# A two-stage transformer kernel on one core: the feed-forward half's second product from fp32r parts, and where weights and rotation tables are loaded

## The chip, the cores and the metric

The kernel runs on one core of one Trainium2 chip. Its time is the device time of one execution in microseconds; the median of several runs counts. Engines are TensorE (PE, with its weight loads as PEld), VectorE (DVE), ScalarE (ACT), GpSimd (POOL) and SyncE (SP), which issues most transfers.

## What is computed

An attention layer without a mask over 2 x 2048 tokens (256 wide, 16 heads of 16), then two layers of local attention and a gated feed-forward half. In float32, cut to what matters:

```python
def _layer(x, wqkv, qs, ksc, wo, lg, lb, w1, b1, w2, b2):      # twice, DEPTH = 2
    h = shift_token(x)                                          # half of the columns from the token before
    q, k, v = split(h @ wqkv)                                   # 8 heads of 64
    q, k = rotary_xpos(l2norm(q) * qs, l2norm(k) * ksc)         # rotation tables by position
    x = x + local_attention(q, k, v) @ wo                       # windows of 128, the one before and its own
    h = layer_norm(shift_token(x)) * lg + lb
    a, g = split(h @ w1 + b1)                                   # 682 columns each
    h = a * gelu(g)
    return x + h @ w2 + b2                                      # w2: 682 x 256
```

## The kernel before

The program has three phases: projection of the first attention, its attention (32 heads, to about 1500 us), and `feed_forward_phase`, which runs the end of the first attention and both local layers, to 2903 us. The order of the work on each engine is written out by hand: every engine has its own loop over `steps`, and semaphores tie them together.

In the third phase a tile is 128 tokens; there are `NT` = 32 tiles a layer and 64 in all. Step `t` handles several tiles at different stages: on TensorE in turn the scores of tile `t + 1` (`scores`, L1222), the projection of `t + 2` (`project`, L1191), the transposes of the probabilities of `t + 1` (L1261), the transpose of the normalised rows of `t` (L1237), outputs of heads of `t + 1` (L1303), transposes of queries and keys of `t + 2` (L1326, which waits for `rotary_done`), the product with `wo` of `t + 1` (L1342), and the transpose of `x` for `t + 3` (L1175).

The feed-forward half is done for a pair of tiles. In an even step TensorE does the first product, `hidden` (L1289), of the pair that begins with `t - 2`: 36 matmuls behind the scores and 30 behind L1237. ScalarE applies the gelu (L1468, L1470) and DVE multiplies (`gated`, L1676); the result, `act_T`, stands in `gate`, six chunks of 256 tokens, of which the last has 64 rows. In the odd step that follows TensorE does the second product, `hidden_out` (L1358), once for each tile of the pair: `hidden_out(t - 3)` behind the scores and `hidden_out(t - 2)` behind L1237. It multiplies `gate` with `w2_sb`, both float32 (the trace shows each such matmul as two instructions). `add_hidden` (L1615) on DVE adds the product to `x_sb`.

The first product and the projection already work with parts: a value is rounded to fp32r ("hi"), the rest is a second fp32r value ("lo"), and hi x hi, hi x lo and lo x hi are summed, three fp32r matmuls for one. Weights are split into such parts by GpSimd during the attention phase, in pieces of 512 columns (`PIECES`, `split_piece`, L556 and L558), and stored in DRAM; SP moves them (`prepare_weights`). The pieces pass through the space of `tables`, where the rotation's cosines and sines are loaded afterwards as a whole (`load_tables`).

The second layer's `wqkv` is loaded in two halves: the high part by SP at the start of the phase, into its own space in `k_stack` (`load_second_wqkv(sp, 0)`), the low part by ScalarE's queue over the first layer's low part, once the first layer's last projection is done (`t + 2 == NT - 1`).

On DVE the step's order is: maxima of the scores (L1584), split of the transposed `x` (L1603), reciprocals (L1592), statistics of the middle rows (L1622 to L1627, which wait for a DMA that shifts rows of `x_mid`), normalisation of two groups of probabilities (L1598), cosines of queries and keys (L1641, both wait for ScalarE's `squares_made`), normalised rows (L1634), copy of transposed probabilities (L1655), square norms (L1649), the second copy, rotation (L1662, L1663), scaling of the keys by the inverse norm (L1669). On ScalarE: exponentials (L1427), copies and squares of queries and keys (L1438, L1439), copies of transposed probabilities (L1448), L1456, in even steps the gelu, then copies L1476, L1481, L1483 and the rounding of transposed `x` (L1488, L1490). On GpSimd: normalisation of two groups of probabilities (L1046), L1051, addition of the bias (L1056), sines (L1067, two instructions), inverse norms (L1074, L1076, a power), the split of the first product's input (L1084, L1086), and every second step the rotation's tables (L1039).

Of the kernel before, what the change touches and what calls it, by code (L numbers as in the profile page):

```python
# [13 lines left out]
P = 128  # L14
# [369 lines left out]
def attention_phase(nc, ins, division, VO, mask_sb, weights, ident, load_output_weights, stacks, qkT_stored):  # L384

    with ExitStack() as ctx:
# [3 lines left out]
        q_stack, k_stack, q_minus_first = stacks.q, stacks.k, stacks.q_minus  # L390
        v_ones = sb("v_ones", [P, BODY, TB, VW])
        probs = sb("probs", [P, PROBS, 512])
        excess = probs[:, PROBS - BLOCKS:].rearrange("p (i k) c -> p i k c", i=2)
        spare_pieces = weights.tables[:].rearrange("p a t h d -> p (a t h d)").rearrange("p (i c) -> p i c", c=PIECE)
        raw_piece, piece_hi, piece_lo = spare_pieces[:, 0], spare_pieces[:, 1].bitcast(F32R), spare_pieces[:, 2].bitcast(F32R)
# [61 lines left out]
        def _(sp):  # L457
# [33 lines left out]
            for n in range(NH):  # L491
# [16 lines left out]
                if n == TABLES_HEAD:  # L508
                    sp.wait_ge(weights.parts_stored, 32 * (len(PIECES) - IN_PLACE))
                    weights.load_tables(sp, ins)  # L510
# [9 lines left out]
        def _(pool):  # L520
# [23 lines left out]
            def split_piece(i):  # L544
# [3 lines left out]
                if i < IN_PLACE:  # L548
                    _, _, k, columns = PIECES[i]
                    hi, lo = weights.wqkv_hi[0][:, k, columns], weights.wqkv_lo[:, k, columns]  # L550
# [154 lines left out]
        def _(dve):  # L705
# [70 lines left out]
          + [("w1", l, k, slice(a, min(a + PIECE, W1_COLUMNS))) for l in range(LAYERS) for k in range(NC) for a in range(0, W1_COLUMNS, PIECE)])  # L776
# [3 lines left out]
class Weights:  # L780


    def __init__(self, nc, ctx, stacks):
# [5 lines left out]
        self.wqkv_hi = [sb("wqkv2_hi0", [P, NC, 3 * INNER], F32R)]  # L789
        self.wqkv_lo = sb("wqkv2_lo", [P, NC, 3 * INNER], F32R)  # L790
        self.tables = sb("tables2", [P, 2, TB, 2, D2 // 2])
# [8 lines left out]
        self.tables_loaded, self.small_loaded = sem("tables2_loaded"), sem("small2_loaded")  # L800
        self.wqkv1_loaded, self.w1_loaded, self.wo_loaded, self.w2_loaded = (sem(n) for n in ("wqkv2_1_loaded", "w1_2_loaded", "wo2_loaded", "w2_loaded"))

    def place_wide(self, ctx, stacks):
# [5 lines left out]
        self.w2 = sb("w2_sb", [P, HC, C])  # L809

    def place_second(self, in_k):

        self.wqkv_hi.append(in_k(NC, 3 * INNER))

    def raw_piece(self, ins, i):
        name, l, k, columns = PIECES[i]
        return ins[name][l].rearrange("(k p) n -> p k n", p=P)[:, k, columns]

    def stored_piece(self, i, part):
        name, l, k, columns = PIECES[i]  # L820
        return self.wqkv_parts[part, :, k, columns] if name == "wqkv2" else self.w1_parts[l, part, :, k, columns]

    def load_tables(self, eng, ins):
        for i, name in enumerate(("cos2", "sin2")):
            eng.dma_start(self.tables[:, i], ins[name].rearrange("(t p) (a d) -> p t a d", p=P, a=2)).then_inc(self.tables_loaded, 16)
# [18 lines left out]
    def load_w2(self, eng, ins, l):  # L844
# [13 lines left out]
def feed_forward_phase(nc, ins, weights, stacks, division, x_sb, outputs, spare, wo1_loaded, x1_dram, mask_sb, ident, out):  # L858

    with ExitStack() as ctx:  # L860
# [162 lines left out]
        def _(pool):  # L1023
# [109 lines left out]
            for t in steps:  # L1133
# [17 lines left out]
                if exists(t):  # L1151
                    split_y(t)
# [749 lines left out]
```

## Time and profile before

| | us |
|---|---|
| median of three runs | 2899.72 |
| the three runs | 2899.66, 2899.72, 2905.52 |
| the profiled execution, whole | 2905.26 |
| its span | 2903.4 |
| busy in it: PE, DVE, ACT, POOL | 2807.7, 2323.1, 2113.7, 960.1 |

A row of a timeline gives the start, the length, the engine and line, the tiles written and read with their shapes, the count of instructions merged into it, and in brackets the idle time before it with what ended it. On TensorE instructions overlap, so that their pace is read from starts and not from lengths. Names are those of the memory, not of the view: `VO` holds queries, keys, probabilities and rotated values, `k_stack` the split of `x`, `q_minus_first` and `q_stack` the first product's operands, `tables_small` small columns and the rotation's tables, `wo_bo_sb` the normalised rows.

### The profile page before, as it was taken

The numbers are of one execution on the slowest core, as the hardware profiler recorded it, in microseconds if no ns is written. First come the engines' busy times: TensorE is split into PE (matmuls) and PEld (weight loads), VectorE is DVE, ScalarE is ACT, GpSimd is POOL, SyncE is SP. The second block draws the span as 40 slices with busy tenths as digits, with TensorE's granted clock in tenths as the row PEclk, the third lists the DMA queues.
The fourth block names the chain that finished last, engine by engine and source line by source line (L and its number), as shares of the span: only waits on it lengthen the run. The fifth ranks groups of instructions, "written<-read, shape, count | busy, mean of one in ns | idle before, by whom it ended". The sixth has DMA issues, their size and how long they took to land. (4 is left out here: it accounts for less than half of the span.)

```text
span 2903.4 us, 59150 instructions
## 1 busy us (share of the span) xinstructions
PE 2807.7 (97%) x22608; PEld 1755.0 (60%) x22608; DVE 2323.1 (80%) x4287; ACT 2113.7 (73%) x4556; POOL 960.1 (33%) x1102
## 2 busy tenths in 40 slices
PE   7999999999999999999997899999999999999997
PEld 7743333333333333333355788888887788888886
DVE  7779999999999999999816677777776677777774
ACT  5568888888888888888856566666666676666763
POOL 7600000010001000000016555555555555656553
PEclk9869999999999999999998899999999999999999
DMA  5613334443444243424203000000000100000000
GB/s 164 189 18 53 52 46 60 62 72 59 70 61 72 55 68 60 74 43 66 42 22 128 11 5 4 5 5 4 5 4 34 54 12 19 19 19 11 20 18 25
DMA packets 85944, 131.33 MB, mean 45 GB/s; under 512 B 33120, under 2 KB 59168, under 8 KB 78240
## 3 DMA queue, kind: packets, MB, share of 16 engines
q1 hardware_dynamic: 79376, 120.41, 21.1%
q10 hardware_dynamic: 6288, 7.14, 0.8%
q8 instruction: 181, 2.97, 0.5%
q14 instruction: 99, 0.81, 0.1%
HBM read 83.98 MB, written 34.61 MB: 41 GB/s over the span
## 5 line engine op out<-in xcount | busy, mean ns | idle before, releaser
L684 ACT ACTIVATE probs<-scores 128x512 f32<-128x512 f32 x2048 | 1114.7, 596 | 199.2 <-PE scores L610 76.3
L717 DVE TENSOR_REDUCE mx<-aux 128x1 f32<-128x1024 f32 x982 | 1201.1, 1223 | 61.4 <-PE aux L578 54.1
L578 PE MATMUL aux<-k_stack,q_stack 48*128 48x512 f32 x2006 | 757.4, 453 | 6.4 <-DMA k_stack<-qk_dram 4.1
L610 PE MATMUL scores<-q_stack,k_stack 50*128 50x512 f32 x2048 | 762.5, 450 | 0.0
L623 PE MATMUL pv<-probs,v_ones 128*32 128x256 f32 x8192 | 658.5, 393 | 0.1
L610 PEld LDWEIGHTS scores<-q_stack,k_stack 50*128 50x128 f32 x2048 | 310.2, 186 | 428.8 <-ACT probs L684 411.2
L623 PEld LDWEIGHTS pv<-probs,v_ones 128*32 128x32 f32 x8192 | 161.7, 108 | 361.5 <-ACT probs L684 289.4
L578 PEld LDWEIGHTS aux<-k_stack,q_stack 48*128 48x128 f32 x2006 | 306.4, 188 | 38.0 <-DVE mx L717 19.2
L531 POOL CAST m_parts<-head_max 128x16 fp32r<-128x16 f32 x32 | 6.3, 198 | 938.6 <-DVE head_max L710 938.6
L1427 ACT ACTIVATE VO<-VO,tables_small 128x256 f32<-128x256 f32 (+1 forms) x512 | 250.9, 492 | 48.7 <-DVE tables_small L1584 48.5
L1289 PE MATMUL bank<-q_minus_first,q_stack 128*128 128x256 f32 x2112 | 268.5, 285 | 0.6 <-DVE x_sb L1615 0.6
L1289 PEld LDWEIGHTS bank<-q_minus_first,q_stack 128*128 128x128 f32 x2112 | 256.5, 191 | 11.0 <-issue 10.9
L1584 DVE CUSTOM_DVE_ANT_0 VO<-bank,mask_sb,tables_small 128x256 f32<-128x256 f32 (+1 forms) x512 | 216.1, 469 | 52.0 <-PE bank L1222 52.0
L1046 POOL TENSOR_TENSOR VO<-VO,tables_small 128x512 f32<-128x512 f32 (+1 forms) x128 | 127.3, 1015 | 347.9 <-DVE tables_small L1592 347.9
L1067 POOL TENSOR_TENSOR VO<-VO,tables_small 128x512 f32<-128x512 f32 x128 | 166.1, 1319 | 99.2 <-issue 99.2
L1358 PE MATMUL bank<-w_sb,gate 128*128 128x256 f32 (+1 forms) x768 | 195.8, 397 | 1.3 <-DVE gate L1676 1.1
L1076 POOL TENSOR_TENSOR tables_small<-tables_small 128x16 f32<-128x16 f32 x64 | 189.6, 2962 | 5.3
L1358 PEld LDWEIGHTS bank<-w_sb,gate 128*128 128x128 f32 (+1 forms) x768 | 137.6, 192 | 47.4 <-issue 31.7
L1191 PE MATMUL bank<-wqkv_lo,k_stack 128*128 128x512 f32 x384 | 152.2, 396 | 0.0
L1476 ACT COPY oT<-bank 128x512 f32<-128x512 f32 x64 | 37.6, 587 | 155.5 <-PE bank L1303 155.5
L1438 ACT COPY VO<-bank 128x512 f32<-128x512 f32 x128 | 75.1, 587 | 83.9 <-PE bank L1191 83.9
L1191 PE MATMUL bank<-wqkv_hi,k_stack 128*128 128x512 f32 x384 | 128.6, 402 | 5.2 <-DVE tables_small L1584 2.7
(173 smaller groups left out, 4334.9 us busy)
## 6 DMA issues: line engine op xcount, KB each, us to landing
q_stack<-qk_dram SPq DMA_DIRECT2D x192, 128.0 KB, 5.1
k_stack<-qk_dram SPq DMA_DIRECT2D x192, 128.0 KB, 7.2
qk_dram<-qkT_hi SPq DMA_DIRECT2D x32, 256.0 KB, 3.7
qk_dram<-qkT_lo SPq DMA_DIRECT2D x32, 256.0 KB, 3.8
VO<-o_stage SPq DMA_DIRECT2D x128, 32.0 KB, 6.9
q_minus_first<-sums_dram SPq DMA_DIRECT2D x32, 128.0 KB, 2.9
w_parts<-tables SPq DMA_DIRECT2D x16, 256.0 KB, 2.5
x_dram<-x_sb SPq DMA_DIRECT2D x16, 256.0 KB, 2.0
```

The lines of the kernel that those rows point to most:

```text
L578: return nc.tensor.matmul(out, q_stack[max_rows, n % BODY, tile * P:(tile + 1) * P], k_stack[max_rows, n % BODY, keys * 512:(keys + 1) * 512],
L610: last = nc.tensor.matmul(out, k_stack[0:SCORE_ROWS, n % BODY, s * P:(s + 1) * P], q_stack[0:SCORE_ROWS, n % BODY, j * 512:(j + 1) * 512], ...
L623: last = nc.tensor.matmul(pv[VW * j:VW * (j + 1), columns], v_ones[:, n % BODY, s, :], probs[:, (BLOCKS * step + j) % PROBS, columns], sta ...
L684: nc.scalar.activation(probs[:, e % PROBS], scores[:, item_of_exp(e) % BANKS1], ACT.Exp, scale=float(D1) ** -0.5).then_inc(act_emptied, 1)
L717: nc.vector.tensor_reduce(mx[:, n % BODY, tile, half:half + 1], aux[:, unit % 2].rearrange("p a k -> p (a k)"), AX.X, ALU.max).then_inc(dv ...
L1067: last = nc.gpsimd.tensor_tensor(out=o4[:, :, :, lo:lo + D2 // 2], in0=q4[:, :, :, hi:hi + D2 // 2], in1=sin_table[:, v // 2 % 2, :, lo:lo ...
L1076: nc.gpsimd.tensor_tensor(out=rnorm[:, v % 2], in0=norm2_min, in1=minus_half, op=ALU.pow).then_inc(rnorm_made, 1)
L1191: last = nc.tensor.matmul(bank[QKV_BANK[a]][:], x_part[:, v % 4, k, tokens], w_part[:, k, columns], start=(k == 0 and n == 0), stop=(k == ...
L1289: last = nc.tensor.matmul(out_half, w_part[:, k, chunk * P:(chunk + 1) * P], h_part[:, p % 2, k], start=(k == 0 and n == 0), stop=(k == NC ...
L1358: last = nc.tensor.matmul(bank[F_BANK[v % 2]][:, 0:C], act_T[rows, c, v % 2 * P:(v % 2 + 1) * P], w2_sb[rows, c], start=(c == 0), stop=(c ...
L1427: last = nc.scalar.activation(probs[j][:, u, keys], probs[j][:, u, keys], ACT.Exp, scale=-1.0, bias=negmax[:, j, u:u + 1], accum_out=sums[ ...
L1584: last = nc.vector.tensor_tensor_reduce(out=probs[j][:, u, at:at + n_keys], in0=src[:, 2 * u * P + at:2 * u * P + at + n_keys], in1=mask_s ...
```

## The change

`w2` is split into parts like the other weights: six more pieces, stored as `w2_parts`, loaded as `w2_hi` and `w2_lo`. `hidden_out` now sums three products (act_hi x w2_hi, act_hi x w2_lo, act_lo x w2_hi), 18 fp32r matmuls for six float32 ones. The parts of the activation are new tiles in `k_stack`: ScalarE rounds `gate` to `act_hi` in two halves of three chunks (`round_hidden`), and GpSimd subtracts (`split_hidden`). The missing rows of the last chunk are zeroed once. `gelu` of a pair waits for the subtraction of the pair before, where it waited for its second product.

To make room, the second layer's `wqkv` has no space of its own: both parts are loaded by ScalarE's queue in the layer change, over the first layer's. The pieces have a buffer of their own (`weight_pieces`), and the rotation's tables only hold two pairs: SP loads those of a pair in the odd step `t` for pair `(t + 5) // 2`.

```diff
+PIECES ... + [("w2", l, None, slice(a, a + PIECE)) for l in range(LAYERS) for a in range(0, HC * C, PIECE)]
...
-        act_T = gate
+        act_hi, act_lo = in_k(HC, 2 * P), in_k(HC, 2 * P)
...
             weights.load_first(sp, ins)
-            weights.load_second_wqkv(sp, 0)
             for t in steps:
+                if t % 2 == 1 and exists(t + 5):
+                    p = (t + 5) // 2
+                    sp.wait_ge(tables_made, 2 * (p - 1))
+                    weights.load_tables(sp, ins, p)
...
             def rotary_tables(p):
+                pool.wait_ge(weights.tables_loaded[p % 2], 32 * (p // 2 + 1))
...
+            def split_hidden(p):
+                for i in range(2):
+                    chunks = slice(i * HC // 2, (i + 1) * HC // 2)
+                    pool.wait_ge(act_high_made, 2 * p + i + 1)
+                    nc.gpsimd.tensor_tensor(out=act_lo[:, chunks], in0=gate[:, chunks], in1=act_hi[:, chunks], op=ALU.subtract).then_inc(act_split, 1)
...
             def hidden_out(v):
-                pe.wait_ge(act_made, HC * (v // 2 + 1))
...
-                for c in range(HC):
-                    rows = slice(0, P if c < HW else HR)
-                    last = nc.tensor.matmul(bank[F_BANK[v % 2]][:, 0:C], act_T[rows, c, v % 2 * P:(v % 2 + 1) * P], w2_sb[rows, c], start=(c == 0), stop=(c == HC - 1))
+                out, tokens = bank[F_BANK[v % 2]][:, 0:C], slice(v % 2 * P, (v % 2 + 1) * P)
+                for i, (a_part, w_part) in enumerate(((act_hi, w2_hi), (act_hi, w2_lo), (act_lo, w2_hi))):
+                    for c in range(HC):
+                        if c % (HC // 2) == 0 and i != 1:
+                            pe.wait_ge(act_high_made if i == 0 else act_split, 2 * (v // 2) + c // (HC // 2) + 1)
+                        rows = slice(0, P if c < HW else HR)
+                        last = nc.tensor.matmul(out, a_part[rows, c, tokens], w_part[rows, c], start=(i == 0 and c == 0), stop=(i == 2 and c == HC - 1))
...
             def gelu(p):
-                        act.wait_ge(F_done, 2 * p)
+                        act.wait_ge(act_split, 2 * p)
...
+            def round_hidden(p, i):
+                chunks = slice(i * HC // 2, (i + 1) * HC // 2)
+                act.wait_ge(act_made, HC * p + chunks.stop)
+                if i == 0 and p:
+                    act.wait_ge(F_done, 2 * p)
+                nc.scalar.copy(act_hi[:, chunks], gate[:, chunks]).then_inc(act_high_made, 1)
...
                     if t + 2 == NT - 1:
-                        weights.load_second_wqkv(act, 1)
+                        weights.load_second_wqkv(act)
```

On TensorE, in the odd step, in the kernel before: the scores, the early second product and the first projection matmuls.

```order
L1175 MATMUL bank<-ident,x_sb 128x128 x2
L1222 MATMUL bank<-VO,qT 128x256 x8
L1358 MATMUL bank<-w_sb,gate 128x256 x6
L1191 MATMUL bank<-wqkv_hi,k_stack 128x512
L1191 MATMUL bank<-wqkv_lo,k_stack 128x512
```

The same place on TensorE in the changed kernel:

```order
L1190 MATMUL bank<-ident,x_sb 128x128 x2
L1237 MATMUL bank<-VO,qT 128x256 x8
L1376 MATMUL bank<-w_hi,k_stack 128x256 x6
L1376 MATMUL bank<-w_lo,k_stack 128x256 x6
L1376 MATMUL bank<-w_hi,k_stack 128x256 x6
L1206 MATMUL bank<-wqkv_hi,k_stack 128x512
L1206 MATMUL bank<-wqkv_lo,k_stack 128x512
```

Nothing moved here; one row of six became three rows of six, the activation's parts being in `k_stack`.

On ScalarE, from the gelu of an even step to the load of the exponential's table, in the kernel before (at the layer change, where a weight load on this queue also stands):

```order
L1468 ACT_TABLE_LOAD
L1468 ACTIVATE gate<-bank,b_sb 128x256 x5
L1470 ACTIVATE gate<-bank,b_sb 64x256
L1476 COPY oT<-bank 128x512
L1481 COPY qT<-bank 128x512
L1483 COPY VO<-bank 128x512
L1488 CAST k_stack<-bank 128x2x128
L1490 CAST k_stack<-bank 128x1
L838 DMA wo_sb<-in_wo 128x4x256
L1427 ACT_TABLE_LOAD
```

The same place on ScalarE in the changed kernel:

```order
L1486 ACT_TABLE_LOAD
L1486 ACTIVATE gate<-bank,b_sb 128x256 x5
L1488 ACTIVATE gate<-bank,b_sb 64x256
L842 DMA q_stack<-w_parts 128x2816 x2
L1502 COPY oT<-bank 128x512
L1507 COPY qT<-bank 128x512
L1509 COPY VO<-bank 128x512
L1497 CAST k_stack<-gate 128x768
L1514 CAST k_stack<-bank 128x2x128
L1516 CAST k_stack<-bank 128x1
L1497 CAST k_stack<-gate 128x768
L1445 ACT_TABLE_LOAD
```

Two casts of 128x768 were put in, one ahead of the rounding of `x` and one between it and the load of the exponential's table.

On GpSimd, from the end of an even step to the odd step's first instructions, in the kernel before:

```order
L1084 CAST q_minus_first<-wo_bo_sb 128x2x128
L1086 TENSOR_TENSOR q_minus_first<-wo_bo_sb,q_minus_first 128x2x128
L1046 TENSOR_TENSOR VO<-VO,tables_small 128x512 x2
L1051 TENSOR_TENSOR tables_small<-tables_small 128x1
L1056 TENSOR_TENSOR x_sb<-x_mid,q_minus_first 128x256
```

The same place on GpSimd in the changed kernel:

```order
L1090 CAST q_minus_first<-wo_bo_sb 128x2x128
L1092 TENSOR_TENSOR q_minus_first<-wo_bo_sb,q_minus_first 128x2x128
L1099 TENSOR_TENSOR k_stack<-gate,k_stack 128x768 x2
L1052 TENSOR_TENSOR VO<-VO,tables_small 128x512 x2
L1057 TENSOR_TENSOR tables_small<-tables_small 128x1
L1062 TENSOR_TENSOR x_sb<-x_mid,q_minus_first 128x256
```

The two subtractions stand between the split of an even step and the normalisation of the odd one.

## Rows read from the trace of the kernel before

**Rows 1.** Busy time by stretch, one of a hundred microseconds in the settled part
```profile
1900.00:2000.00 100.00, 98.84 (x733) 84.71 (x733) 71.97 (x208) 64.11 (x166) 55.04 (x57) 1.00 0.02 5
```

Its columns are the stretch, its length, busy time of PE, PEld, DVE, ACT and POOL with their instructions, granted clock, DMA share and GB/s.

**Rows 2.** TensorE's timeline over one odd step
```profile
2135.91 2.00 PE L1222 MATMUL bank<-VO,qT 64*128 64x256 f32 x16
2137.84 3.05 PE L1358 MATMUL bank<-w_sb,gate 128*128 128x256 f32 x12
2140.82 0.50 PE L1191 MATMUL bank<-wqkv_hi,k_stack 128*128 128x512 f32 x1
...
2147.09 2.97 PE L1358 MATMUL bank<-w_sb,gate 128*128 128x256 f32 x12
...
2152.34 1.09 PE L1326 MATMUL bank<-ident,VO 128*128 128x128 f32 x8 [0.39 <-DVE VO L1669]
...
2155.31 2.00 PE L1222 MATMUL bank<-VO,qT 64*128 64x256 f32 x16
```

**Rows 3.** TensorE's waits from 1560 us on: total, times, longest
```profile
PE bank L1326 <- DVE VO L1669: 17.2, 33, 2.3
```

**Rows 4.** DVE's timeline in the same odd step
```profile
2144.06 0.68 DVE L1641 TENSOR_TENSOR VO<-bank,tables_small 128x512 f32<-128x512 f32 x1
2145.05 0.69 DVE L1641 TENSOR_TENSOR VO<-bank,tables_small 128x512 f32<-128x512 f32 x1 [0.31 <-ACT VO L1439]
2145.66 0.43 DVE L1634 TENSOR_SCALAR wo_bo_sb<-x_mid,tables_small 128x256 f32<-128x256 f32 x1
2146.20 0.69 DVE L1655 COPY PT<-bank 128x512 f32<-128x512 f32 x1
...
2151.49 0.80 DVE L1669 TENSOR_TENSOR VO<-VO,tables_small 128x512 f32<-128x512 f32 x1 [1.67 <-POOL tables_small L1076]
```

**Rows 5.** TensorE's timeline in the even step before
```profile
2116.81 4.56 PE L1289 MATMUL bank<-q_minus_first,q_stack 128*128 128x256 f32 x36
2121.21 0.39 PE L1191 MATMUL bank<-wqkv_hi,k_stack 128*128 128x512 f32 x1
```

**Rows 6.** ScalarE's timeline around the odd step; last row, a group by line
```profile
2134.11 0.59 ACT L1483 COPY VO<-bank 128x512 f32<-128x512 f32 x1
...
2136.47 1.28 ACT L1427 ACT_TABLE_LOAD   x1
2138.00 0.51 ACT L1427 ACTIVATE VO<-VO,tables_small 128x256 f32<-128x256 f32 x1 [0.25 <-DVE tables_small L1584]
...
2142.53 0.59 ACT L1438 COPY VO<-bank 128x512 f32<-128x512 f32 x1 [0.43 <-PE bank L1191]
...
2143.93 0.59 ACT L1438 COPY VO<-bank 128x512 f32<-128x512 f32 x1 [0.31 <-PE bank L1191]
...
L352 ACT CAST bqkv_parts<-bqkv_sb 128x768 fp32r<-128x768 f32 x1 | 0.8, 826 | 0.0
```

**Rows 7.** GpSimd: one group by line, then single rows of its timeline
```profile
L558 POOL TENSOR_TENSOR tables<-tables 128x512 fp32r<-128x512 f32 x14 | 18.0, 1286 | 1.1
...
2858.42 0.74 POOL L1086 TENSOR_TENSOR q_minus_first<-wo_bo_sb,q_minus_first 128x256 fp32r<-128x256 f32 x1
...
2151.82 1.05 POOL L1086 TENSOR_TENSOR q_minus_first<-wo_bo_sb,q_minus_first 128x256 fp32r<-128x256 f32 x1
...
2140.14 2.04 POOL L1046 TENSOR_TENSOR VO<-VO,tables_small 128x512 f32<-128x512 f32 x2 [6.99 <-DVE tables_small L1592]
```

**Rows 8.** A transfer's issue (KB, us to landing); DVE's timeline in step 34
```profile
wqkv_lo<-wqkv_parts ACTq DMA_DIRECT2D x1, 1536.0 KB, 6.4
...
2288.69 0.49 DVE L1622 BATCH_NORM_STATS2 tables_small<-x_mid 128x6 f32<-128x128 f32 x2 [3.72 <-DMA x_mid<-x_mid]
```

**Rows 9.** GpSimd's sines of rows 4's step; DVE and GpSimd at the layer change
```profile
2144.64 2.58 POOL L1067 TENSOR_TENSOR VO<-VO,tables_small 128x512 f32<-128x512 f32 x2 [1.06 <-issue]
...
2269.53 1.39 DVE L1634 TENSOR_SCALAR wo_bo_sb<-x_mid,tables_small 128x256 f32<-128x256 f32 x1
...
2267.82 2.95 POOL L1067 TENSOR_TENSOR VO<-VO,tables_small 128x512 f32<-128x512 f32 x2
```

More of the change, by code:

```diff
@@ L390, in attention_phase @@
         q_stack, k_stack, q_minus_first = stacks.q, stacks.k, stacks.q_minus
+        pieces = sb("weight_pieces", [P, 3, PIECE])
         v_ones = sb("v_ones", [P, BODY, TB, VW])
@@ L508, in _ @@
                 if n == TABLES_HEAD:
-                    sp.wait_ge(weights.parts_stored, 32 * (len(PIECES) - IN_PLACE))
-                    weights.load_tables(sp, ins)
+                    for p in range(2):
+                        weights.load_tables(sp, ins, p)
                 if n == TABLES_HEAD + 1:
@@ L799, in __init__ @@
         self.b2_dram, self.b2_copied = nc.dram_tensor("b2_copy", (LAYERS, C), F32).ap(), sem("b2_copied")
-        self.tables_loaded, self.small_loaded = sem("tables2_loaded"), sem("small2_loaded")
+        self.tables_loaded, self.small_loaded = [sem(f"tables2_loaded{i}") for i in range(2)], sem("small2_loaded")
         self.wqkv1_loaded, self.w1_loaded, self.wo_loaded, self.w2_loaded = (sem(n) for n in ("wqkv2_1_loaded", "w1_2_loaded", "wo2_loaded", "w2_loaded"))
@@ L842, in load_w1, with load_w2 @@
             eng.dma_start(self.w1[part].bitcast(F32), self.w1_parts[l, part]).then_inc(self.w1_loaded, 16)
-    def load_w2(self, eng, ins, l):
-        eng.dma_start(self.w2[:], ins["w2"][l].rearrange("(k p) n -> p k n", p=P)).then_inc(self.w2_loaded, 16)
+    def load_w2(self, eng, l):
+        for part in range(2):
+            eng.dma_start(self.w2[part][:].rearrange("p k n -> p (k n)").bitcast(F32), self.w2_parts[l, part]).then_inc(self.w2_loaded, 16)
     def load_first(self, eng, ins):
@@ L1152, in _ @@
                     split_y(t)
+                if t % 2 == 0 and exists(t - 2):
+                    split_hidden((t - 2) // 2)
                 if exists(t + 3) and (t + 3) % 2 == 0:
@@ L1182, in project @@
                     pe.wait_ge(weights.wqkv1_loaded, 32)
-                hi, lo = wqkv_hi[layer(v)], wqkv_lo
+                hi, lo = wqkv_hi, wqkv_lo
                 for a in range(3):
@@ L1348, in hidden_out @@
                 if v % NT == 0:
[L1349 to L1350 removed]
+                    pe.wait_ge(weights.w2_loaded, 32 * (layer(v) + 1))
                 if v % 2 == 0:
@@ L1558, in _ @@
                     copy_qT_kT(t + 2)
+                if t % 2 == 0 and exists(t - 2):
+                    round_hidden((t - 2) // 2, 0)
                 if t >= 0 and exists(t + 3):
                     round_xT(t + 3)
+                if t % 2 == 0 and exists(t - 2):
+                    round_hidden((t - 2) // 2, 1)
                 p = finished_pair(t)
```

58 lines of the change are left out of this document (30 added, 28 removed).

## The prediction, made before the changed kernel ran

> **What bounds the kernel now.** I read the busy time by stretch first, then TensorE's timeline over two steps of the feed-forward phase, then its waits, then the other three engines' timelines over the same step. In the settled part of the phase TensorE is busy 98.84 of 100 us at full granted clock [rows 1]. So taking work from TensorE pays, unless something else is as late as it is. The reader is to look for that something in the one step that the change shortens.
>
> Steps come in pairs. The even step of a pair holds a pair's first product (`hidden`), the odd one both second products (`hidden_out`): one right behind the scores, at 2137.84, one behind the transposes, at 2147.09 [rows 2]. The odd step is 19.4 us long, scores to scores (2135.91 to 2155.31) [rows 2]. Behind its late product TensorE waits 0.39 us, until 2152.34, for DVE's scaled keys [rows 2]; such waits are 17.2 us in all, 33 times, the largest entry of its list [rows 3]. In the even step it never waits there. So the odd step has a second chain that already ends last.
>
> That chain does not pass through the late product. It starts at the projection of the tile two ahead and runs: ScalarE's copy and square of the keys, DVE's cosines (L1641, 2145.05), its normalisation (L1634, 2145.66), a copy of probabilities (L1655, 2146.20), square norms, GpSimd's power, DVE's scaling (L1669, 2151.49), TensorE's L1326 [rows 4]. From 2146.20 to 2152.34 (6.14 us) nothing in it waits for a product.
>
> **The change part by part.**
>
> *The product itself.* Before, 12 instructions in 2.98 us (2137.84 to 2140.82); the late one, at 2147.09, shows 2.97 [rows 2]. After, 18 fp32r instructions of the form 128x128 by 128x256, the form of L1289: 36 of these take 4.40 us (2116.81 to 2121.21), 0.122 us each [rows 5]. 18 x 0.122 = 2.20 us. So each product is 0.75 us shorter (two a pair, 64 in all, 48 us of TensorE time).
>
> *The late product's 0.75 us* is lost: it lies ahead of the 0.39 us wait, which becomes about 1.1 us. Gain 0.
>
> *The early product's 0.75 us* moves the projection forward by that, and the chain hangs on the projection; what else is it late for? DVE: it runs without a pause from the scores' maxima to the first cosines at 2144.06 [rows 4]. The start-to-start time of such an instruction is about 0.61 (2145.05 to 2145.66), so DVE is free for the second cosines at 2144.67 and not before. Today it starts them at 2145.05 after 0.31 us of idling for ScalarE. Then L1634 at 2145.28, and L1655 0.35 later at 2145.63 (its transpose would be there at 2146.20 - 0.75 = 2145.45). That is 0.57 us earlier than 2146.20, and the rest of the chain follows: **gain 0.57 us an odd step**, not 1.5.
>
> *ScalarE's two roundings* (`round_hidden`, 128x768 each, once a pair). A cast of 128x768 took 0.826 us; the next instruction starts some 0.1 us before such an end (as DVE's 2145.05 is 0.69 long and followed at 0.61 [rows 4]), so about 0.70 of the engine each [rows 6]. The first stands behind the keys' copy of 2134.11 and ends at 2135.4, where the engine waited for TensorE anyway. The second stands ahead of the load of the exponential's table, 1.28 us at 2136.47; exponentials began at 2138.00 after a short wait for DVE [rows 6]. Now: 2136.47 + 0.70 + 1.28 = 2138.45, that is 0.45 later. The engine idled 0.43 us before the queries' copy of 2142.53 [rows 6], so it is free at 2142.10 + 0.45 = 2142.55. Copy, square, then the keys' copy at 2143.53 instead of 2143.93, its square done at 2144.6: just ahead of the 2144.67 at which DVE is free. Cost nil beside DVE, with 0.05 us to spare; from there each further 0.1 us on ScalarE takes 0.1 from the gain.
>
> *GpSimd's two subtractions* (`split_hidden`, 128x768). 128x512 took 1.286, 128x256 alone 0.74: 2.13 ns an element, so 1.83 us each [rows 7]. The first can run 2135.5 to 2137.3, the second 2137.35 to 2139.2, where GpSimd stood idle until 2140.14 (normalisation) [rows 7]. TensorE wants the second one after 15 of the early product's 18 matmuls: 2137.84 + 1.83 = 2139.67. Covered by 0.45 us. The other bound: beside DVE's scaling the 256 form took 1.05, not 0.74 [rows 7]; at 4.1 ns an element that is 3.15 us each. I take 1.83, because what DVE runs from 2135.5 to 2139.2 reads PSUM and one SBUF operand, where the slowed row stood beside a product of two SBUF operands.
> The Trainium skill (SBUF — State Buffer, Who interferes with whom) says that GpSimd and DVE share a port pair under an exclusive lock, taken by DVE instructions with two SBUF inputs or in a two-port mode only. By that rule the sum stays at 1.83; by the slowed row taken for all of DVE's instructions it would be the second rival below.
>
> *Waits.* `gelu` now waits for the subtraction of the pair before, a step old: nil. GpSimd's queue behind the subtractions holds only the next normalisation, due at 2140.14: nil while they end before. The second rounding has only the table load behind it.
>
> *Tables pair by pair.* Two 32 KB loads on SP in odd steps, ahead of the next shift of `x_mid`; the wait before them is for tables made two steps earlier, and their reader comes two steps later. Nil.
>
> *Six more weight pieces* in the attention phase: six subtractions of 1.29 us [rows 7] and six casts on GpSimd, which idles there (its busy share is 0 to 1 tenth in those slices of the page); nil, as for the 24 before.
>
> *One-off places.* (a) Opening: 0.75 MB less ahead of the first shift; at the pace of (b) 3.2 us of transfer: gain 0 to 3, I take 1. (b) `wqkv` whole at the layer change: the low half landed in 6.4 us [rows 8]; both, sent at 2185.7, land within 13 us, by 2199, and the projection needs them at 2202. Nil, or 1 us if it hits a shift. (c) Second-layer `w2` is 1.5 MB for 0.75; DVE already waited 3.72 us at 2288.69 for a shift behind it [rows 8]; another 0.75 MB is about 2 us more: loss 2. (d) The end: the last pair's rounding (0.8) and subtraction (1.8) stand in the open, less 1.5 us of TensorE: loss 1.
>
> *Sum.* 31 x 0.57 = 17.7 gained, 2 to 3 us lost net in the one-off places: **15.5 us less**. Against the profiled execution (span 2903.4, run 2905.3) that gives 2889.8. Of the three runs shown two lie at 2899.7 and one at 2905.5, as the profiled one; against the median 2899.7 it gives **2884**.
>
> **The rivals.**
>
> 1. *All of TensorE's time counts*: 31 x 1.5 = 46 us, 2854. It needs the second chain to have slack, and the wait of 0.39 us in every odd step says that it has none. 5%.
>
> 2. *The subtractions come too late* (slower). At 3.15 us each the second ends at 2141.8, the product at 2142.15 instead of 2140.82, and projection, DVE's addition of the product and the chain follow: 1.3 us x 31 = +41, 2940. At 2.6 us each it is +0.4 x 31 = 2912. It decides from where both together take over 4.9 us. 8%.
>
> 3. *DVE misses its turn beside GpSimd* (slower). L1634 starts 1.02 us after GpSimd's sines (L1067, 2.58 us for two), inside the first of them, and takes 0.43. At the layer change it came at 2269.53, 1.71 behind, just past the first, and took 1.39 [rows 9]: shut out by the second. The sines follow the keys' copy, L1634 follows DVE. If the copy is early by all of TensorE's 0.75 (ScalarE not held up as I reckon), the sines start at 2143.9 and L1634 comes at 2145.28, 1.4 later, past the first's end at 1.29; it is then done near 2146.5 to 2146.8 and L1655 is 0.25 to 0.55 later than today: +8 to +17, 2907 to 2917. By my times the sines start at 2144.24 and L1634 comes 1.04 later, 0.25 us inside. Since the margin is small: 15%. The page named above has this rule, that whoever is second waits for the whole instruction; the 1.39 us agree.
>
> 4. *ScalarE takes the gain*: if the second rounding and the table load hold it 0.35 to 0.6 us longer than I reckon, the keys' square is last and 0 to 0.2 us a step remain: 31 x 0 to 0.2 less the 2.5 us of the one-off places, 2896 to 2902. 10%.
>
> Forecast as worked out: 62%, own range 2874 to 2894 (gain per step 0.3 to 0.8, one-off places by 4 us either way, and whether the runs fall low or 6 us high).
>
> **Numbers.** Predicted 2884. The range 2872 to 2908 holds the forecast, rival 4 and the lower end of rival 3; left out are rivals 1 and 2 and the rest of 3. A measurement of this kernel tells about 0.2% (6 us) from no change. Faster by more: forecast and rival 1, less the forecast's edge: 0.65. Within: rival 4 and edges: 0.13. Slower: rivals 2 and 3 with theirs: 0.22.
>
> **What would show it.** Right: the odd step near 18.8 us (scores to scores) for 19.4, the even one unchanged; TensorE's wait at L1326 near 1.3 us in each odd step, 40 us in all; DVE's second cosines with no idle time before them; no wait of the second product for GpSimd; subtractions near 1.83. Wrong: a wait inside the early product (rival 2), L1634 over 1 us long in odd steps (rival 3), DVE idle before the second cosines (rival 4), or no wait at L1326 (rival 1).

## The result, and the profile after

The changed kernel is slower: 2925.5 us median of five runs (2918.0 to 2929.0) against 2899.7 us (2897.0 to 2905.5), a ratio of 1.0083 with a 95% interval of [1.0063, 1.0103]. The forecast was 2884 us, its range 2872 to 2908. The profiled execution of the changed kernel has a span of 2923.7 us, 20.3 us more than that of before (25.8 by the medians: the profiled execution of before took 2905.3 us).

Only a part of these spans bears on the change. The time from the first scores to the end is 1342.1 us before and 1361.6 us in the changed kernel, 19.4 more. A kernel that differs from before in the order of the first product alone (e3_before_spread) has 1342.5. The time ahead of the first scores, in which the change adds little but the splitting of `w2`, goes from 1552.8 to 1575.1 us in the ten traces of this case, at a mean granted clock of 0.99 in the shortest and 0.97 in the longest. Of the 7.1 us between the traces of before and of e3_before_spread 6.8 lie there. So single steps are compared by the traces, and whole times by the ratios of many runs.

In the changed kernel `scores` is L1237, the first product L1304, the projection L1206, the second product L1376, the transposes of the rotated keys L1341, `split_hidden` L1099, `round_hidden` L1497. TensorE's timeline over one odd step (start, length, engine and line, tiles, count; the projection's rows lie between the early product's three rows and the late one's, of which the first stands here):

```profile
2140.36 2.00 PE L1237 MATMUL bank<-VO,qT 64*128 64x256 f32 x16
2142.28 1.17 PE L1376 MATMUL bank<-w_hi,k_stack 128*128 128x256 f32 x6
2143.38 1.16 PE L1376 MATMUL bank<-w_lo,k_stack 128*128 128x256 f32 x6
2144.47 1.16 PE L1376 MATMUL bank<-w_hi,k_stack 128*128 128x256 f32 x6
...
2151.76 1.15 PE L1376 MATMUL bank<-w_hi,k_stack 128*128 128x256 f32 x6
...
2155.02 1.20 PE L1318 MATMUL bank<-PT,VO 128*64 128x128 f32 x18
```

Six matmuls of the product take 1.10 us (2142.28 to 2143.38), 0.183 each, where `hidden`'s take 0.122 [rows 5]. The early product takes 3.29 us (the next projection matmul starts at 2145.57) instead of 2.98 [rows 2], the late one 3.26 (2151.76 to 2155.02) instead of 2.90. The forecast was 2.20. So the product from fp32r parts is longer than the float32 one.

The weight loads show why. Rows of TensorE's weight loads in the same early product, each read in a window of its own, so that a load can stand in two of them (x2): the last two full chunks, the last chunk (64 rows), and the first two of the next part:

```profile
2142.63 0.30 PEld L1376 LDWEIGHTS bank<-w_hi,k_stack 128*128 128x128 f32 x2
...
2142.75 0.19 PEld L1376 LDWEIGHTS bank<-w_hi,k_stack 128*128 128x128 f32 x1
...
2143.07 0.18 PEld L1376 LDWEIGHTS bank<-w_hi,k_stack 64*128 64x128 f32 x1
...
2143.38 0.30 PEld L1376 LDWEIGHTS bank<-w_lo,k_stack 128*128 128x128 f32 x2
```

Loads of full chunks start 0.12 us apart (2142.63, 2142.75). The 64-row chunk's load starts 0.32 us behind its predecessor, and the next 128-row one 0.31 us behind it. At 0.117 these two distances would be 0.23 together; they are 0.63. One visit to the 64-row chunk between chunks of 128 rows, called a stay here, costs 0.40 us, and the part-by-part order makes three stays in a product: 18 x 0.117 + 3 x 0.40 = 3.3 us.

The waits tell the same. One of TensorE's waits (total, times, longest) in the changed kernel, over the whole trace:

```profile
PE bank L1341 <- DVE VO L1699: 7.1, 5, 2.3
```

Over the whole trace of before the wait for the scaled keys was 18.4 us in 34 times; it is 7.1 in 5. (From 1560 us on it was 17.2 in 33 [rows 3], and it is 5.9 in 4.) The late product, 0.36 us longer, has eaten the 0.39 us of each odd step.

Where the 20.3 us are, from the starts of the scores in the two traces: +0.30 in each of 28 settled odd steps (8.4), 0.00 to 0.02 in the even ones; +3.3 in the odd step of the layer change, +0.2 in the next odd one; +2.5 in the step behind the second layer's `w2` load; +5.1 behind the last scores; +0.7 in the opening and ahead of it; some 0.2 in even steps and rounding.

### The profile page after: what moved, and what is told of

The parts are those of the page before. It is cut to its first block and busy times, and to the rows that moved or that the text cites. A ratio compares the mean times of both kernels' runs of the same rounds, so it can differ in the third digit from the quotient of the medians.

```text
span 2923.7 us, 60204 instructions
## 1 busy us (share of the span) xinstructions
PE 2835.1 (97%) x22992; PEld 1784.6 (61%) x22992; DVE 2324.0 (79%) x4287; ACT 2160.8 (74%) x4620; POOL 1087.3 (37%) x1179
## 5 line engine op out<-in xcount | busy, mean ns | idle before, releaser
L1304 PE MATMUL bank<-q_minus_first,q_stack 128*128 128x256 f32 x2112 | 271.7, 287 | 0.6 <-DVE x_sb L1645 0.6
L1304 PEld LDWEIGHTS bank<-q_minus_first,q_stack 128*128 128x128 f32 x2112 | 259.7, 193 | 10.9 <-issue 10.8
L1206 PE MATMUL bank<-wqkv_hi,k_stack 128*128 128x512 f32 x768 | 256.4, 401 | 6.7 <-DVE tables_small L1614 4.1
L1206 PEld LDWEIGHTS bank<-wqkv_hi,k_stack 128*128 128x128 f32 x768 | 145.4, 189 | 43.2 <-issue 4.3
L1376 PE MATMUL bank<-w_hi,k_stack 128*128 128x256 f32 (+1 forms) x768 | 152.2, 318 | 2.3 <-ACT k_stack L1497 1.4
L1206 PE MATMUL bank<-wqkv_lo,k_stack 128*128 128x512 f32 x384 | 152.2, 396 | 0.0
L1099 POOL TENSOR_TENSOR k_stack<-gate,k_stack 128x768 fp32r<-128x768 f32 x64 | 116.7, 1844 | 89.5 <-ACT k_stack L1497 89.5
```

The lines of the kernel that those rows point to most:

```text
L1206: last = nc.tensor.matmul(bank[QKV_BANK[a]][:], x_part[:, v % 4, k, tokens], w_part[:, k, columns], start=(k == 0 and n == 0), stop=(k == ...
L1304: last = nc.tensor.matmul(out_half, w_part[:, k, chunk * P:(chunk + 1) * P], h_part[:, p % 2, k], start=(k == 0 and n == 0), stop=(k == NC ...
L1376: last = nc.tensor.matmul(out, a_part[rows, c, tokens], w_part[rows, c], start=(i == 0 and c == 0), stop=(i == 2 and c == HC - 1))
```

## The experiments

Two theories stood against each other. **Height**: what costs is changing between weights (stationary operands) of 128 and of 64 rows. **Load**: a matmul whose stationary operand is not that of the one before costs 0.183 us (`hidden` uses `w1_hi` twice running, so its mean would be 0.122). A third: these matmuls are slow for where their operands lie.

### All 128 rows in the last chunk: e5_full_rows

```diff
-                        rows = slice(0, P if c < HW else HR)
+                        rows = slice(0, P)
```

> The changed kernel, with all 128 rows of the last chunk of the activation and of w2 in the second product (rows 64 to 127 are zeros in all of them). Theory H (height): in the trace of the changed kernel the weight loads inside a part product start every 0.117 us, but the load of the 64-row chunk starts 0.32 us after its predecessor, and the next 128-row one 0.31 us after it: 0.40 us for each stay at 64 rows, three of them in a product. Without them a product should take 18 x 0.117 = 2.1 us instead of 3.3, each odd step should be about 0.57 us shorter than before the change (the chain over VectorE then sets it, as predicted), and TensorE should wait about 1.1 us for the scaled keys in it. One-off places stay: 2899.7 + 11 - 31 x 0.57 = about 2893. Rival L (load): a matmul whose stationary operand isn't that of the one before it costs 0.183 us, so the product stays at 3.3 and the time at 2925. Rival O: these matmuls are slow for their operands' place, also 2925.

Measured: 2885.0 us, ratio to the kernel before 0.9932 [0.9910, 0.9954], and the odd step is 0.69 to 0.74 us shorter than before in 26 of the 28 settled ones. The expectation of 2893 was too high: the step gained more than 0.57, and part of the changed kernel's losses at the layer change and the end are gone too. Loads, TensorE and its wait:

```profile
2136.59 0.19 PEld L1376 LDWEIGHTS bank<-w_hi,k_stack 128*128 128x128 f32 x1
2136.70 0.19 PEld L1376 LDWEIGHTS bank<-w_lo,k_stack 128*128 128x128 f32 x1
...
2146.37 0.19 PEld L1376 LDWEIGHTS bank<-w_hi,k_stack 128*128 128x128 f32 x1
2146.69 0.14 PEld L1318 LDWEIGHTS bank<-PT,VO 128*64 128x64 f32 x2
...
2149.77 1.09 PE L1341 MATMUL bank<-ident,VO 128*128 128x128 f32 x8 [1.11 <-DVE VO L1699]
...
PE bank L1341 <- DVE VO L1699: 39.2, 34, 2.3
```

The last chunk of one part is followed by the first of the next after 0.11 us (2136.59, 2136.70); from the first of the 18 loads to the one behind the last it is 2.12 us (2136.00 to 2138.12), and from matmul to matmul 2.23. The wait at L1341 is 39.2 us in all; the prediction said 40 for a 2.20 us product. Height holds; load and place fall, since neither order nor place was changed.

The third and fourth row show a limit of the name. Behind the late product, now 128 rows throughout, come the outputs of heads (L1318), whose weights have 128 rows and 64 columns. Their first load starts 0.32 us behind the last full chunk's, as one of 64 rows does. So the change to weights of 64 columns costs as much as one of the rows: loads of 128 x 128 that follow others of that shape from another line (L1252, then L1376) are 0.11 us apart in the changed kernel, so it is not the change of line. No run varies the columns alone. For this the late product, to the start of L1318, takes 2.32 us and not 2.12. VectorE's timeline in the same step:

```profile
2142.12 1.28 DVE L1671 TENSOR_TENSOR VO<-bank,tables_small 128x512 f32<-128x512 f32 x2
2143.32 0.40 DVE L1664 TENSOR_SCALAR wo_bo_sb<-x_mid,tables_small 128x256 f32<-128x256 f32 x1
2143.64 0.68 DVE L1685 COPY PT<-bank 128x512 f32<-128x512 f32 x1
```

Both cosines run without a pause (x2), the normalisation takes 0.40 us and is not shut out, and the copy starts 9.56 us behind the scores (2134.08); before it was 10.29 (2146.20 less 2135.91) [rows 2, 4]. That is 0.73 us, against a forecast of 0.57: the 0.57, 0.11 for first cosines that come 8.04 instead of 8.15 us behind the scores, and a few hundredths behind them.

### The 64-row chunk once a product: e2_by_chunk

```diff
-                for i, (a_part, w_part) in enumerate(((act_hi, w2_hi), (act_hi, w2_lo), (act_lo, w2_hi))):
-                    for c in range(HC):
-                        if c % (HC // 2) == 0 and i != 1:
-                            pe.wait_ge(act_high_made if i == 0 else act_split, 2 * (v // 2) + c // (HC // 2) + 1)
-                        rows = slice(0, P if c < HW else HR)
+                for c in range(HC):
+                    if c % (HC // 2) == 0:
+                        pe.wait_ge(act_split, 2 * (v // 2) + c // (HC // 2) + 1)
+                    rows = slice(0, P if c < HW else HR)
+                    for i, (a_part, w_part) in enumerate(((act_hi, w2_hi), (act_hi, w2_lo), (act_lo, w2_hi))):
```

> The changed kernel, with the second product summed chunk by chunk: the three part products of a chunk stand together, so that the 64-row chunk comes once, last. Theory H: 18 x 0.117 + 0.40 = 2.5 us a product. The second subtraction of GpSimd is then wanted after 9 matmuls instead of 15, about 0.3 us before it is there, so the odd step is about 0.15 us shorter than before the change: about 2906. Rival L: 12 new stationary operands x 0.183 = 2.2 us. Rival O: 3.3 us and 2925.

Measured: ratio 1.0013 [0.9996, 1.0030], odd step 0.04 us shorter than before. The loads at the end of an early product (the rows of the second 64-row load left out), the late product's ends, and the wait:

```profile
2143.95 0.19 PEld L1376 LDWEIGHTS bank<-w_hi,k_stack 128*128 128x128 f32 x1
...
2144.28 0.18 PEld L1376 LDWEIGHTS bank<-w_hi,k_stack 64*128 64x128 f32 x1
...
2144.50 0.18 PEld L1376 LDWEIGHTS bank<-w_hi,k_stack 64*128 64x128 f32 x1
...
2144.82 0.19 PEld L1206 LDWEIGHTS bank<-wqkv_hi,k_stack 128*128 128x128 f32 x1
...
2151.01 0.37 PE L1376 MATMUL bank<-w_hi,k_stack 128*128 128x256 f32 x1
...
2153.50 1.97 PE L1318 MATMUL bank<-PT,VO 128*64 128x128 f32 x32
...
PE bank L1376 <- POOL k_stack L1099: 10.6, 34, 3.3
```

Three 64-row loads in a row are 0.11 us apart (2144.28 to 2144.50, two distances), with 0.33 before and 0.32 behind: it is the change that costs, not 64 rows. The late product takes 2.49 us, as expected from one stay. The early one takes 2.95 (2141.87 to 2144.82), since it stands 0.45 us longer between its third and fourth chunk for GpSimd's second subtraction, which this order wants after 9 matmuls instead of 15. Little of the gain is left: expected 0.15 us a step, found 0.04.

### Two stays a product: e1_pairs

```diff
-                for i, (a_part, w_part) in enumerate(((act_hi, w2_hi), (act_hi, w2_lo), (act_lo, w2_hi))):
+                for lo in (False, True):
...
+                        for w_part in ((w2_hi,) if lo else (w2_hi, w2_lo)):
+                            last = nc.tensor.matmul(out, (act_lo if lo else act_hi)[rows, c, tokens], w_part[rows, c],
+                                                    start=(not lo and c == 0 and w_part is w2_hi), stop=(lo and c == HC - 1))
```

> The changed kernel, with the two products of the activation's high part side by side for each chunk, then the low part's products of all chunks: two stays at 64 rows instead of three. Theory H: 18 x 0.117 + 2 x 0.40 = 2.9 us a product, as long as before the change: odd steps equal those of before, time about 2911. Rival L: 12 x 0.183 = 2.2 us, time near 2893. Rival O: 3.3 us and 2925.

Measured: ratio 1.0015 [0.9990, 1.0041], odd step 0.08 us shorter than before. A late product of this kernel, its last full chunk, the stay, the low part's chunks and what follows:

```profile
2137.29 0.28 PE L1377 MATMUL bank<-w_lo,k_stack 128*128 128x256 f32 x1
2137.50 0.38 PE L1377 MATMUL bank<-w_hi,k_stack 64*128 64x256 f32 x1
2137.72 0.27 PE L1377 MATMUL bank<-w_lo,k_stack 64*128 64x256 f32 x1
2137.92 1.16 PE L1377 MATMUL bank<-w_hi,k_stack 128*128 128x256 f32 x6
2139.01 1.97 PE L1318 MATMUL bank<-PT,VO 128*64 128x128 f32 x32
```

It takes 2.87 us (2136.14 to 2139.01), where height says 2.9 and load 2.2. With three, two and one stay the late product takes 3.26, 2.87 and 2.49 us: 0.38 for each. With none (e5_full_rows) it takes 2.32, only 0.17 less than with one: a last stay that is followed by the 64-column weights of L1318 has one change on its way out (0.31 us), and without it the change to 64 columns is still there (0.32).

### `hidden` without a repeated operand: e3_before_spread

```diff
-                            for n, (w_part, h_part) in enumerate(((w1_hi, hT_hi), (w1_hi, hT_lo), (w1_lo, hT_hi))):
+                            for n, (w_part, h_part) in enumerate(((w1_hi, hT_hi), (w1_lo, hT_hi), (w1_hi, hT_lo))):
```

> The kernel before, with the three part products of the feed-forward half's first product in another order: w1_hi x hT_hi, w1_lo x hT_hi, w1_hi x hT_lo, so that the stationary operand (w1) is never that of the matmul before it. Its result is the same sum. Theory H: nothing changes, 36 matmuls in 4.4 us, time within 3 us of before. Rival L: 0.183 us instead of 0.122 for each of 66 matmuls a pair, 4.0 us a pair, about 129 us more: 3029.

Measured: ratio 1.0000 [0.9983, 1.0017]. The first product's 36 matmuls take 4.42 us, for 4.40 before:

```profile
2123.90 4.58 PE L1289 MATMUL bank<-q_minus_first,q_stack 128*128 128x256 f32 x36
2128.32 0.39 PE L1191 MATMUL bank<-wqkv_hi,k_stack 128*128 128x512 f32 x1
```

A new stationary operand of 128 x 128 for every matmul costs nothing beside a moving one of 256 columns. The load theory falls. The trace of before could have settled it alone: its 2112 matmuls at L1289 have 2112 weight loads, so a repeated operand was loaded again there too.

### Only the late product with 128 rows: e8_late_full

```diff
-                        rows = slice(0, P if c < HW else HR)
+                        rows = slice(0, P if c < HW or v % 2 else HR)
```

> The changed kernel, with 128 rows in the late product of each pair only; the early one keeps its 64-row chunk. If the late product lies ahead of a wait, as the prediction says, its 1.2 us turn into a wait for the scaled keys (about 1.2 us in each odd step) and the odd steps stay 0.30 us longer than before the change: 2920 to 2925, ratio about 1.007. If all TensorE time counted, 31 x 1.2 = 37 us less than the changed kernel, ratio 0.995.

Measured: ratio 1.0052 [1.0028, 1.0077]; odd steps +0.30 us, as in the changed kernel.

```profile
2170.83 1.09 PE L1341 MATMUL bank<-ident,VO 128*128 128x128 f32 x8 [1.07 <-DVE VO L1699]
...
PE bank L1341 <- DVE VO L1699: 38.9, 34, 2.4
```

The late product takes 2.30 us for 3.26, 0.96 less, and the gain stands in the wait (1.07 us in this step), not in the step. In the settled steps its length is free as long as a wait is left behind it. By the ratios this kernel is not told from the changed one (1.0052 and 1.0083, with intervals that overlap). Between the two traces there are differences at two places: the odd step of the layer change is +0.31 us here and +3.25 in the changed kernel, and the time from the last scores to the end is 56.0 us here, 60.8 in the changed kernel and 55.7 before. In both places TensorE partly runs at 1.2 GHz, the lower of its two levels. The changed kernel at the layer change, then this one:

```profile
2235.05 1.94 PE L1376 MATMUL bank<-w_hi,k_stack 128*128 128x256 f32 x6
...
2240.66 1.97 PE L1318 MATMUL bank<-PT,VO 128*64 128x128 f32 x16
2242.57 1.97 PE L1341 MATMUL bank<-ident,VO 128*128 128x128 f32 x8
```
```profile
2248.64 1.65 PE L1376 MATMUL bank<-w_hi,k_stack 128*128 128x256 f32 x6
...
2252.43 1.09 PE L1318 MATMUL bank<-PT,VO 128*64 128x128 f32 x16
```

The product takes 5.61 us in the one and 3.79 in the other, and behind it the transposes (L1341, 1.97 against the usual 1.09) are still slow in the changed kernel. Over 2232 to 2242 its granted clock is 0.62; before, over 2228 to 2238, it was 0.83. Why the full clock comes back later there stays open, and each kernel has one trace only. That the stays are its cause is not shown: with two of them (e1_pairs) the late product at the layer change ran at full clock (2.90 us) and the step was 0.22 us longer than before, while with full rows (e5_full_rows) that product took 4.13 us.

### Before, with 128 rows: e7_before_full

```diff
+            nc.gpsimd.memset(gate[HR:P, HW], 0.0).then_inc(columns_made, 1)
+            pool.wait_ge(columns_made, 3)
...
-                    rows = slice(0, P if c < HW else HR)
+                    rows = slice(0, P)
```

> The kernel before, unchanged in loads and in the float32 product, but the last chunk's matmul takes 128 rows (its rows 64 to 127 zeroed once). In the trace of before the stay at 64 rows costs 0.52 - 0.11 going in and 0.52 - 0.22 coming out, some 0.6 to 0.7 us a product. If the early product's time counts as the prediction's chain says, 0.55 to 0.6 us less in each odd step and none in the even one: 31 x 0.57 = 18 us, ratio 0.994, and TensorE's wait for the scaled keys grows from 0.4 to about 1.0 us. If all TensorE time counted, 31 x 1.3 = 40 us, ratio 0.986. If the height were not what costs, no change.

Measured: 2894.1 us, ratio 0.9966 [0.9947, 0.9985], odd step 0.39 us shorter.

Weight loads of before around the early product's 64-row chunk, then this kernel's products:

```profile
2139.45 0.41 PEld L1358 LDWEIGHTS bank<-w_sb,gate 128*128 128x128 f32 x2
2140.19 0.29 PEld L1358 LDWEIGHTS bank<-w_sb,gate 64*128 64x128 f32 x2 [0.33 <-issue]
2140.82 0.19 PEld L1191 LDWEIGHTS bank<-wqkv_hi,k_stack 128*128 128x128 f32 x1 [0.33 <-issue]
```
```profile
2127.79 2.86 PE L1360 MATMUL bank<-w_sb,gate 128*128 128x256 f32 x12
2130.30 0.58 PE L1193 MATMUL bank<-wqkv_hi,k_stack 128*128 128x512 f32 x1
...
2136.65 2.78 PE L1360 MATMUL bank<-w_sb,gate 128*128 128x256 f32 x12
2139.36 1.97 PE L1305 MATMUL bank<-PT,VO 128*64 128x128 f32 x32
```

In before the full chunks' loads start 0.22 us apart, the first 64-row one 0.52 us behind the last full one, and the projection's 0.52 us behind the second 64-row one. Here the early product takes 2.5 us for 2.98, and the first two projection matmuls give 0.1 back. The step gains 0.39, less than my 0.55 to 0.6: I had counted each gap of the 64-row chunk whole, though its two loads then follow one another in 0.11 us where a full chunk's take 0.22. What the early product gives, the step gives, up to the limit that VectorE sets (0.57, and 0.71 with the rest); the late product's gain (2.71 us for 2.90) is lost again. By the ratios, about half of what the full rows gain over before (0.9932) can be had without splitting `w2`.

### The loads alone: e4_loads_only

```diff
-        act_hi, act_lo = in_k(HC, 2 * P), in_k(HC, 2 * P)
+        act_T = gate
...
-        self.w2 = tuple(sb(f"w2_{part}", [P, HC, C], F32R) for part in ("hi", "lo"))
+        self.w2 = sb("w2_sb", [P, HC, C])
```

> The changed kernel's loads (wqkv whole at the layer change, rotation's tables pair by pair, a buffer of its own for the pieces) with the float32 second product and unsplit w2 of the kernel before. It prices the loads alone: by the prediction nothing (at most 1 us), ratio 1.000; the odd steps equal those of before. If the 11 us of one-off places in the changed kernel came from wqkv and the tables, 2910 and 1.004; if from w2's second megabyte and the product's own length at low clock, none of it shows here.

Measured: ratio 0.9991 [0.9972, 1.0010], odd steps equal to those of before, the layer change's step equal to 0.01 us. `wqkv` whole at the layer change, the tables pair by pair and the separate buffer cost nothing that the runs can tell (the time from the first scores to the end is 1.1 us longer in its trace).

### Loads behind the exponentials: e6_late_loads

This kernel has the full rows of e5_full_rows as well.

```diff
-                        rows = slice(0, P if c < HW else HR)
+                        rows = slice(0, P)
...
+                if exists(t + 1):
+                    exponentials(t + 1)
                 if t == NT - 1:
                     act.wait_ge(Y_done, NT)
                     weights.load_wo(act, ins, 1)
                 if t == NT + 2:
                     act.wait_ge(F_done, NT)
                     weights.load_w2(act, 1)
-                if exists(t + 1):
-                    exponentials(t + 1)
```

> The changed kernel with 128 rows in the product, and the second layer's wo and w2 issued by ScalarE behind the exponentials of their step instead of ahead of them, so that SyncE's shift of x_mid is queued first. With the loads ahead, VectorE waited 3.06 and 5.56 us for the shift at those places. Theory: both waits shrink to those of an ordinary step, some 1 and 2.5 us less than with the full rows alone relative to before plus what before itself lost to its own 3.72 us wait: 3 to 6 us less than the full rows alone, ratio to before 0.991 to 0.992. Rival: the shift waits for something else, or the later loads hit the next consumer: same as the full rows alone, 0.993.

Measured: 2882.4 us, ratio to the kernel before 0.9925 [0.9903, 0.9947]. VectorE's statistics of the middle rows behind the `w2` load, with the full rows alone and here:

```profile
2287.57 0.49 DVE L1652 BATCH_NORM_STATS2 tables_small<-x_mid 128x6 f32<-128x128 f32 x2 [5.56 <-DMA x_mid<-x_mid]
```
```profile
2275.21 0.49 DVE L1652 BATCH_NORM_STATS2 tables_small<-x_mid 128x6 f32<-128x128 f32 x2 [0.24 <-DMA x_mid<-x_mid]
```

The wait goes from 5.56 to 0.24 us. The step behind `w2` is 2.1 us shorter than before instead of 1.8 longer, the layer change's 2.1 shorter instead of 0.6 longer: 6.5 us between the two traces, 0.7 of it given back in the step between them; from the first scores to the end it is 1319.2 us for 1325.6. The medians differ by less, 0.9932 to 0.9925 of their own before's, and the intervals overlap. That the wait is gone is shown, and so are the shorter steps in one trace each; that the whole time is shorter for it is not. By its ratio this is the lowest of the kernels, though not told from the full rows alone.

## Why the prediction was wrong

**The failed step is the price of the product.** The prediction took 18 x 0.122 us from `hidden` as "the form of L1289" [rows 5]. `hidden` has 128 rows in every matmul. In the product three of 18 have 64, and they stand apart. The sum needed 3 x 0.40 more: 3.3 us instead of 2.20, a product longer than before instead of shorter. The sign of the whole forecast hung on that term. Rows 2 had a hint that I did not weigh: of 12 matmuls in 2.98 us, at the 0.216 that the full chunks' matmuls of that same product lie apart, 12 would be 2.6, so 0.4 us were already the one stay's. The weight loads of before show it singly (0.52 us in and 0.52 out, under e7_before_full). The part-by-part order, written out in the change, triples it.

**The chain was right.** Given a product of 2.2 to 2.3 us (e5_full_rows), the odd step is 0.71 us shorter (forecast 0.57), the wait at L1341 39.2 us (40), the cosines have no pause, the even step is unchanged to 0.02, and the whole is 20 us below before (forecast 15.5; the interval of the ratio is 13 to 26, and the traces give 16.6 from the first scores on). That the late product's length is free was shown by e8_late_full, and that the early one's counts by e7_before_full and e5_full_rows.

Two readings of the prediction were slightly off without weight in the result. The late product of before takes 2.90 us by its pace (2.97 is a row's length), so its share was 0.70 and not 0.75. And in rival 2 subtractions of 2.6 us each would end at 2140.7 and the product at 2141.07, 0.25 us late and not 0.4, so 2907 and not 2912.

**Beside it.** ScalarE's roundings and GpSimd's subtractions, all 64 of each, in the changed kernel:

```profile
L1497 ACT CAST k_stack<-gate x64: 827/832/846, 1650.5 to 2906.5; 128x768 fp32r<-128x768 f32 x64
...
L1099 POOL TENSOR_TENSOR k_stack<-gate,k_stack x64: 1824/1843/1874, 1651.4 to 2908.5; 128x768 fp32r<-128x768 f32 x64
```

0.83 us at each rounding and 1.84 (forecast 1.83) at each subtraction (least, median and greatest ns), none slowed beside VectorE, and in the settled steps no wait of the product for them. So rival 2 didn't occur, nor rival 4. Rival 3 occurred in no settled step of the changed kernel. With the shorter product it occurred in two: with the full rows the normalisation took 1.40 us in the odd step at 2351.12, and the step was 0.5 us longer than before instead of 0.7 shorter; one other settled step (at 1665.81, 1.41 us) was like it. Elsewhere the margin held, at 2143.32 with 0.40 us.

**The one-off places.** (a) The opening's third step was 1.5 us shorter, its first 1.4 longer: nil for a forecast of 1. The 1.5 is in every trace with the changed loads, the 1.4 only in three of the seven (this one, e4_loads_only and e8_late_full), 0.1 in the others; why was not looked for. (b) `wqkv` and tables: nil, as forecast (e4_loads_only). (c) `w2`: 2.45 us for 2, and e6_late_loads shows that it is the shift queued behind the load. (d) The end: 5.1 us for 1. The waits there are as foreseen, 1.42 us for the rounding and 0.58 for the subtraction. What was missed is that the late product, with its three stays, runs at 1.2 GHz there (1.87 us for six, 5.6 in all) and that the last pair's first product behind it stayed slow, 10.43 us for the 8.15 of before. Before, then the changed kernel:

```profile
2878.99 8.15 PE L1289 MATMUL bank<-q_minus_first,q_stack 128*128 128x256 f32 x66 [0.61 <-DVE x_sb L1615]
```
```profile
2888.56 1.93 PE L1376 MATMUL bank<-w_hi,k_stack 128*128 128x256 f32 x6
2890.42 1.94 PE L1376 MATMUL bank<-w_lo,k_stack 128*128 128x256 f32 x6
2892.29 1.94 PE L1376 MATMUL bank<-w_hi,k_stack 128*128 128x256 f32 x6
2894.84 10.43 PE L1304 MATMUL bank<-q_minus_first,q_stack 128*128 128x256 f32 x66 [0.61 <-DVE x_sb L1645]
2906.69 1.55 PE L1376 MATMUL bank<-w_hi,k_stack 128*128 128x256 f32 x6 [1.42 <-ACT k_stack L1497]
...
2910.44 1.89 PE L1376 MATMUL bank<-w_hi,k_stack 128*128 128x256 f32 x9 [0.58 <-POOL k_stack L1099]
```

The same at the layer change, 3.3 us for 0. In the traces of the kernels with fewer stays in the late product both are smaller: +0.2 to +0.6 at the layer change (e6_late_loads aside, whose loads stand elsewhere) and at most +1.7 behind the last scores; +0.3 and +0.3 in e8_late_full. Why is open, as said there. Together 11.6 us more than before in these places, where 2 to 3 were forecast.

No rival named this cause. The 22% for slower stood on mechanisms that the runs show to be rare or absent; a rival "the matmul's price is not that of `hidden`" was missing, though it was the largest term taken from another line.

## What to carry to other kernels

Take a matmul's price only from one with the same rows, the same columns and the same neighbours, and look at the single weight loads, not at a mean. Where a ragged last chunk is summed in several passes, give it all 128 rows with zeros, or put its passes side by side. On an engine that looks full, ask of each stretch which wait it stands ahead of: shortening the early product paid, shortening the late one did nothing in the settled steps.

## What the runs showed of the hardware

- Changing the height of the stationary operand from 128 to 64 rows and back costs 0.38 to 0.40 us at full clock (loads 0.32 and 0.31 us apart for 0.117). From weights of 128 columns to the next line's of 64 it is as much (0.32 us apart, e5_full_rows; no run varies the columns alone), and in the float32 product a change of either kind shows as 0.52 for 0.22 (before, e7_before_full). Between 64-row loads of the same rows there is no such gap (0.11 us), nor within the scores, whose 64-row loads come in pairs, one for each half of the rows, 0.01 us apart (16 matmuls in 1.92 us).
- The Trainium skill (TensorE: Matmul & The Clock Gate, The mechanism) says in its list that a weight load overlaps with running matmuls only when it goes to other row groups. Ahead of that list the same section also lets loads into a background weight buffer go ahead. Here loads into the same 128 rows start every 0.117 us beside matmuls of 0.28 us: the first sentence taken alone does not hold here, and the second fits. In this product the loads that don't keep the pace are those at a change of rows, and the one behind it at a change of columns. Where page and trace differ, the measurement decides.
- An fp32r matmul of 128x128 by 128x256 sustains one per 0.117 to 0.122 us, whether its stationary operand is that of the one before or not (e3_before_spread).
- A float32 one is two instructions, 0.216 us each, 0.43 together.
- A 1.5 MB weight load issued just ahead of a small shift delayed it until VectorE had waited 5.56 us; the same load issued behind it, 0.24.
